# A graph network's second self connection, moved beside the edges of its layer

## The chip, the cores and the metric

The kernel runs on one core of a Trainium2 chip. The metric is the time on the device in microseconds (us), the median of several runs. The engines are called PE (TensorE, with its weight loads as PEld), DVE (VectorE), ACT (ScalarE), POOL (GpSimd) and SP (SyncE, which here only issues DMAs).

## The reference

A graph of 50,000 nodes with 160 features each (64 scalars, 32 vectors of 3) and 25,000 edges sorted by destination goes through two layers of a tensor product convolution. After each layer stands a residual and a layer norm. Cut to the second layer, which the change touches:

```python
sc = concatenate([x0 @ Wsc0 * a * inv8,
                  (einsum('num,uv->nvm', x1, Wsc1) * a[..., None] * inv32).reshape(n, 3 * MUL1)], axis=1)
f0, f1 = x0 @ Wl1_0 * a * inv8, einsum('num,uv->nvm', x1, Wl1_1) * a[..., None] * inv32
e0, e1 = f0[edge_src], f1[edge_src]
...                                     # messages from e0, e1 and the edge's weights, mean by destination
alpha = scal @ Wa * a * inv96
out_s = scal @ Wl2_s * a * inv96
out_v = einsum('num,uv->nvm', vec, Wl2_v) * a[..., None] * inv96
return sc + alpha * concatenate([out_s, out_v.reshape(n, 3 * MUL1)], axis=1)
...
x = layernorm(x + layer0(x)); x = layernorm(x + layer1(x))
```

The self connection `sc` needs only the layer's input x (in the kernel `x1_rows`, the output of the first layer) and the node's attribute `a`. So does the residual.

## The kernel before, in words

All numbers are fp32. The kernel has four stages, one after the other: edges of layer 0, nodes of layer 0, edges of layer 1, nodes of layer 1. An edge stage goes over 98 pairs of 128 edges, a node stage over 98 groups of 512 nodes (four node tiles of 128, `T = 4`).

The helper `run_stages` (line 59) writes out the order of every engine by hand: for each step k it calls a list of functions, each with its lag, so that `(3, second_map)` handles pair k - 3. The engines take their lists strictly in order and meet only in semaphores.

An edge stage, for pair j:

- SP loads the source indices, the edge scalars and the row of destinations (`load_src`, `load_attr`, `load_dst_row`); in layer 0 it also clears the table of layer 1 in `clear_table1` (L366).
- POOL gathers the source rows with two indirect DMAs (`gather`, L438). Seven steps later it adds the pair's sums into a table in HBM with two indirect DMAs that accumulate (`scatter`, L453). A scatter waits until the previous pair's scatter has landed, because the two can hit the same row.
- PE turns the gathered rows (`turn_x`, L526, L527), maps them (`first_map`, L542, L543), makes the edge's weights (`hidden`, `edge_weights`, L550), turns the products (`turn_mid`, L559), maps them (`second_map`, L573, L575, in layer 0 also L578) and sums edges of equal destination (`sum_pair`, L590 to L592).
- ACT copies out of PSUM (`copy_sums` is L710). DVE makes the products (`products`, L807 and on) and compares destinations. In `choose_rows` (L883, L884, in layer 1 L886) it picks the row to add to, for which it waits until the scatter of two pairs before has landed.

The node stage of layer 1, for group g: SP loads four tiles of x1 (`load_x1`) and of the table (`load_table`). ACT brings z together (`copy_z1`, L729). PE turns x1 (`turn1`, L627, L628) and multiplies it with the self weights (`nodes1`, in `self_connection`, L603 and L605). ACT copies the turned tiles (L735, L736). DVE adds the self connection times `a` to x1 (L930, four a group), takes the reciprocal of the edge count, adds the table's part (`table_row1`, L944) and takes statistics (`stats_of`, L952). POOL makes the factor (`factor`, L493 to L497) and the norm's scale and shift (`powers`, L470 to L485, 10 small operations of 128x4 elements). ACT normalises (L743) and stores `y`.

The buffers of x1 are a ring of four (`x1g`). Between the stages stands one wait for all stores of x1 (`s_store`): on POOL ahead of its first gather of layer 1, and on SP ahead of the last stage's loads.

## Time and profile before

| | us |
|---|---|
| median of 3 runs | 2438.08 |
| lowest and highest | 2436.28 and 2440.83 |
| span of the profiled execution, first to last instruction | 2446.7 |
| POOL busy in it | 1751.4 (72%) |
| PE busy | 1726.5 (71%) |
| DVE busy | 1506.3 (62%) |
| ACT busy | 1070.8 (44%) |

The profiled execution is its own run; its time is the span, some 8.6 us above the median of the runs. The profile names each instruction by engine, line and the tensors that it writes and reads. "Idle before, releaser" is the time in which the engine did nothing ahead of an instruction, and whose semaphore ended it. Matmuls are pipelined and their ends are modelled, so that a busy PE is not PE at its peak. PEclk is the TensorE clock that the chip granted, as a share of full speed (1.0 is 2.4 GHz, 0.5 is 1.2 GHz). The layer 0 edges run to about 860 us, its nodes to 1302, the layer 1 edges to about 2018 and its nodes to the end.

### The profile page before, as it was taken

The numbers are of one execution on the slowest core, as the hardware profiler recorded it, in microseconds if no ns is written. First come the engines' busy times: TensorE is split into PE (matmuls) and PEld (weight loads), VectorE is DVE, ScalarE is ACT, GpSimd is POOL, SyncE is SP. The second block draws the span as 40 slices with busy tenths as digits, with TensorE's granted clock in tenths as the row PEclk, the third lists the DMA queues.
The fourth block names the chain that finished last, engine by engine and source line by source line (L and its number), as shares of the span: only waits on it lengthen the run. The fifth ranks groups of instructions, "written<-read, shape, count | busy, mean of one in ns | idle before, by whom it ended". The sixth has DMA issues, their size and how long they took to land. (4 is left out here: it accounts for less than half of the span.)

```text
span 2446.7 us, 50266 instructions
## 1 busy us (share of the span) xinstructions
PE 1726.5 (71%) x10412; PEld 1528.8 (62%) x10412; DVE 1506.3 (62%) x6121; ACT 1070.8 (44%) x3336; POOL 1751.4 (72%) x3148
## 2 busy tenths in 40 slices
PE   0478888888888666666665878678777766666664
PEld 0367776777776566666664767567666655556564
DVE  1266666666666468888883444444444427888886
ACT  0233333333333246666663333333333325566665
POOL 1066677766667568888884777777777757888887
PEclk9988889888888788888875888988798878878877
DMA  5975555555555467777772444444444436666664
GB/s 223 422 198 121 117 117 117 119 117 116 118 118 119 77 202 252 240 244 243 240 221 69 71 67 69 70 70 69 69 68 69 70 53 226 234 232 235 230 236 175
DMA packets 270387, 374.52 MB, mean 153 GB/s; under 512 B 62544, under 2 KB 172944, under 8 KB 267280
## 3 DMA queue, kind: packets, MB, share of 16 engines
q1 hardware_dynamic: 163264, 203.38, 28.8%
q0 software_dynamic: 75264, 67.79, 19.3%
q10 hardware_dynamic: 31824, 102.97, 10.4%
q8 instruction: 11, 0.18, 0.0%
q14 instruction: 24, 0.20, 0.0%
HBM read 202.83 MB, written 171.16 MB: 153 GB/s over the span
## 5 line engine op out<-in xcount | busy, mean ns | idle before, releaser
L453 POOL DMA_INDIRECT table<-sums,row_i x392 | 632.9, 1615 | 307.0 <-ACT sums L710 104.1
L743 ACT ACTIVATE y<-res,shift,rstd 128x160 f32<-128x160 f32 x784 | 343.8, 509 | 307.4 <-POOL shift L485 307.3
L695 ACT COPY msg<-ps 128x192 f32<-128x192 f32 (+1 forms) x196 | 57.4, 293 | 620.3 <-PE ps L592 437.1
L438 POOL DMA_INDIRECT xg<-in_x_rows,src_i x196 | 199.3, 1017 | 172.2 <-DMA src_i<-in_src_col 69.7
L603 PE MATMUL ps<-self_m,xT 128*128 128x160 f32 (+1 forms) x1568 | 303.8, 350 | 7.6 <-DVE tab L901 4.6
L526 PE MATMUL ps<-ident,xg 128*128 128x128 f32 x392 | 94.1, 325 | 293.1 <-ACT xz L682 214.8
L603 PEld LDWEIGHTS ps<-self_m,xT 128*128 128x128 f32 x1568 | 266.7, 239 | 17.2 <-issue 5.3
L526 PEld LDWEIGHTS ps<-ident,xg 128*128 128x128 f32 x392 | 42.3, 151 | 353.6 <-ACT xz L682 194.4
L438 POOL DMA_INDIRECT xg<-x_rows,src_i x196 | 195.5, 997 | 70.8 <-issue 62.9
L573 PE MATMUL ps<-mapA,midT 128*128 128x128 f32 (+1 forms) x784 | 189.1, 329 | 50.3 <-DVE msg L848 47.8
L483 POOL TENSOR_TENSOR rstd<-var_e,minus_half 128x4 f32<-128x4 f32 x196 | 203.7, 1039 | 15.4
L952 DVE BATCH_NORM_STATS2 stats<-res 128x6 f32<-128x160 f32 x784 | 194.8, 308 | 6.1 <-POOL shift L485 6.0
L573 PEld LDWEIGHTS ps<-mapA,midT 128*128 128x128 f32 x784 | 145.2, 231 | 72.1 <-issue 64.4
L807 DVE TENSOR_TENSOR prod<-hs,ea_all 128x192 f32<-128x192 f32 x196 | 70.2, 358 | 184.5 <-ACT hs L670 163.3
L575 PE MATMUL ps<-mapB,midT 128*128 128x96 f32 x784 | 177.4, 315 | 0.0
L627 PE MATMUL ps<-ident,x1g 128*128 128x128 f32 x392 | 74.9, 322 | 141.6 <-ACT x1z L729 133.7
L618 PE MATMUL ps<-ident,xT 128*128 128x128 f32 x392 | 73.7, 317 | 139.1 <-DVE res L916 138.9
L944 DVE SCALAR_TENSOR_TENSOR res<-tab,small,res 128x160 f32<-128x160 f32 x392 | 124.6, 379 | 69.8 <-POOL small L497 69.7
L886 DVE COPY row_i<-row_all 128x2 int32 (+1 forms) x98 | 17.5, 178 | 237.0 <-DMA table<-sums,row_i 234.9
L559 PE MATMUL ps<-ident,mid 128*128 128x128 f32 x784 | 154.9, 334 | 0.0
L575 PEld LDWEIGHTS ps<-mapB,midT 128*128 128x128 f32 x784 | 150.2, 238 | 0.0
L627 PEld LDWEIGHTS ps<-ident,x1g 128*128 128x128 f32 x392 | 48.5, 160 | 156.9 <-ACT x1z L729 105.6
(121 smaller groups left out, 5019.8 us busy)
## 6 DMA issues: line engine op xcount, KB each, us to landing
tab<-table SPq DMA_DIRECT2D x98, 384.0 KB, 4.2
table<-zeros ACTq DMA_DIRECT2D x24, 1536.0 KB
table<-zeros SPq DMA_DIRECT2D x98, 324.0 KB
tab<-table SPq DMA_DIRECT2D x98, 324.0 KB, 3.3
x_rows<-y ACTq DMA_DIRECT2D x98, 320.0 KB, 3.7
x1g<-x_rows SPq DMA_DIRECT2D x98, 320.0 KB
out_rows<-y ACTq DMA_DIRECT2D x98, 320.0 KB, 2.4
dst_row<-in_dst_row SPq DMA_DIRECT2D x196, 128.0 KB
```

The source lines that it names most:

```text
L438: pool.indirect_dma_start(out=xg[u][:, t, 0:width], out_offset=None, in_=rows, in_offset=bass.IndirectOffsetOnAxis(ap=src_i[u][:, t:t + 1] ...
L453: pool.indirect_dma_start(out=table[l], out_offset=bass.IndirectOffsetOnAxis(ap=row_i[u][:, t:t + 1], axis=0), in_=sums[u][:, t, 0:W], in_ ...
L483: tt(rstd[u][:, :], var_e[:, :], minus_half[:, :], ALU.pow).then_inc(s_rstd, 1)
L526: turn(xgT_ps[:, t, :], xg[u][:, t, 0:M], ident[:, :])
L559: last = turn(midT_ps[:, 2 * c + t, :], mid[u][:, t, c * P:(c + 1) * P], ident[:, :])
L573: mm(o_ps[l][:, t, 0:SO + V], midT[u][:, t, :], mapA[l][:, :], start=t == 0, stop=not L["cross"], skip_group_check=True)
L575: last = mm(o_ps[l][:, t, SO + V:SO + 4 * V], midT[u][:, 2 + t, :], mapB[l][:, :], start=False, stop=not L["cross"], skip_group_check=True)
L603: mm(o[:, t // 2, t % 2, 0:z], xT[u][:, t * P:(t + 1) * P], w_m[:, :], start=True, stop=True)
L627: turn(x1T_ps[u][:, t * P:(t + 1) * P], x1g[u][:, t, 0:M], ident[:, :])
L743: last = nc.scalar.activation(y[u][:, t, :], res[u][:, t, :], ACT.Identity, scale=rstd[u][:, t:t + 1], bias=shift[u][:, t:t + 1])
L944: last = stt(res[u][:, t, :], tab1[u][:, t, 1:161], small[u][:, t, 3:4], res[u][:, t, :], ALU.mult, ALU.add)
L952: last = nc.vector.bn_stats(stats[u][:, t, :], res[u][:, t, :])
```

## The change

The self connection of layer 1, and the residual x1 with it, moves from the last stage into the edge stage of layer 1. In that stage each step k now also handles one node group:

- SP loads x1 of group k (`load_x1`), and four steps later stores its base rows (`store_base`) into a new array `base_rows` in HBM. The load of group k waits until the store of group k - 4 has landed, since both use one buffer of the ring. SP's wait for the stores of x1 now stands ahead of this edge stage.
- ACT brings z together; PE turns and multiplies in two halves of a group (`turn1a`, `turn1b`, `nodes1a`, `nodes1b`) through smaller PSUM tiles; ACT copies the halves (`copy_nTa`, `copy_nTb`); DVE adds them to x1 in place (`add_self_a`, `add_self_b`).
- To free PSUM, the two matmuls of the edge's weights become one of 384 columns over both halves of the edges. `fc2_1` is now 384 wide and block diagonal, cleared first and scaled in four parts.
- The last stage loads the base rows (`load_base`) where it loaded x1. On DVE `residual1` becomes `mean_factor` (two small operations), and `table_row1` adds to the base rows. PE has no work in it, and its warming matmuls are gone.

```diff
@@ sync @@
+                def load_x1(g, m, u):
+                    v = u % 4
+                    wait_count(sp, s_bstore[v], landed(g - 4, first_of(v), 4))
+                    sp.sem_inc(s_sptick, 1)
+                    sp.dma_start(x1g[v][:, :, :].rearrange("p t c -> p (t c)"),
+                                 x1_rows[bass.ds(m * GROUP, GROUP), :].rearrange("(p t) c -> p (t c)", t=T)).then_inc(s_nxT[v], 32)
+                def store_base(g, m, u):
+                    v = u % 4
+                    sp.wait_ge(s_z1, 2 * (g + 1 - NG))
+                    sp.dma_start(base_rows[bass.ds(m * GROUP, GROUP), :].rearrange("(p t) c -> p (t c)", t=T),
+                                 x1g[v][:, :, :].rearrange("p t c -> p (t c)")).then_inc(s_bstore[v], 16)
...
-                run_stages(sp, base, NP, 10, [(0, load_src), (0, load_attr), (4, load_dst_row)] + [(4, clear_table1)] * (l == 0))
+                if l == 1:
+                    for u in range(4):
+                        sp.wait_ge(s_store[u], stored(NG, u))
+                run_stages(sp, base, NP, 10, [(0, load_src), (0, load_attr), (4, load_dst_row)] +
+                           ([(4, clear_table1)] if l == 0 else [(4, store_base), (0, load_x1)]))
...
-                    run_stages(sp, NG, NG, 10, [(0, load_x1), (2, load_table)])
+                    run_stages(sp, NG, NG, 10, [(0, load_base), (2, load_table)])
@@ tensor @@
+                        last = mm(w_ps[1].rearrange("p t c -> p (t c)"), hidT[u][:, :], fc2[1][:, :], start=True, stop=True)
...
+                def turn1(g, b, u):
+                    v = u % 4
+                    pe.wait_ge(s_nxT[v], landed(g, v, 4, 32))
+                    pe.wait_ge(s_x1z, g + 1 - NG)
+                    wait_count(pe, s_nTsb, 2 * (g - NG) + b)
+                    for t in range(2):
+                        turn(x1T_ps[:, t * P:(t + 1) * P], x1g[v][:, 2 * b + t, 0:M], ident[:, :])
+                    turn(z1T_ps, x1z[v][:, 2 * b:2 * b + 2, :], ident[:, :]).then_inc(s_nT, 1)
+                def nodes1(g, b, u):
+                    v = u % 4
+                    pe.wait_ge(s_nTsb, 2 * (g - NG) + b + 1)
+                    wait_count(pe, s_z1, 2 * (g - NG) + b)
+                    for t in range(2):
+                        q = slice((2 * b + t) * P, (2 * b + t + 1) * P)
+                        mm(n1_ps[:, t, 0:M], xT[v][:, q], self_m[1][:, :], start=True, stop=True)
+                    mm(n1_ps[:, :, M:D], z1T[v][:, b, :], self_z[1][0:2 * V, 0:2 * V], start=True, stop=True).then_inc(s_n1, 1)
...
+                    run_stages(pe, NP, NP, 10, [(1, first_map), (0, hidden), (1, edge_weights), (2, nodes1a), (0, turn_x),
+                                                (1, turn1a), (3, second_map), (2, turn_mid), (1, turn1b),
+                                                (2, nodes1b), (5, sum_pair)])
@@ scalar @@
+                    run_stages(act, NP, NP, 10, [(0, copy_z), (1, copy_h), (0, hidden_act), (0, copy_xT),
+                                                 (1, copy_nTa), (3, copy_message), (2, copy_midT), (0, copy_z1),
+                                                 (1, copy_nTb), (5, copy_sums)])
@@ vector @@
+                def add_self(g, m, b, u):
+                    v = u % 4
+                    dve.wait_ge(s_n1, 2 * (g - NG) + b + 1)
+                    for t in range(2):
+                        a = a_all[:, bass.ds(m, 1), 2 * b + t:2 * b + t + 1].rearrange("p g t -> p (g t)")
+                        last = stt(x1g[v][:, 2 * b + t, :], n1_ps[:, t, :], a, x1g[v][:, 2 * b + t, :], ALU.mult, ALU.add)
+                    last.then_inc(s_z1, 1)
...
-                        (4, message_vectors), (4, compare), (4, message_sum), (1, products), (5, choose_rows)])
+                        (4, message_vectors), (4, compare), (4, message_sum), (2, add_self_a), (1, products), (5, choose_rows), (2, add_self_b)])
...
-                    run_stages(dve, NG, NG, 6, [(0, residual1), (1, stats_of), (0, table_row1)])
+                    run_stages(dve, NG, NG, 6, [(0, mean_factor), (1, stats_of), (0, table_row1)])
```

## Rows read from the trace of the kernel before

**Rows 1.** Busy time of the engines in three stages, then PEclk, DMA share, GB/s.

```profile
core 0: us, PE busy (x) PEld busy (x) DVE busy (x) ACT busy (x) POOL busy (x), PEclk, DMA share, GB/s
150.00:850.00 700.00, 585.41 (x3569) 508.97 (x3567) 463.34 (x2292) 261.59 (x907) 483.16 (x365) 0.86 0.55 116
...
1350.00:1960.00 610.00, 468.12 (x2928) 412.48 (x2927) 285.61 (x1241) 228.25 (x796) 460.36 (x353) 0.86 0.47 69
2050.00:2400.00 350.00, 229.29 (x1408) 209.61 (x1409) 289.79 (x1159) 212.98 (x578) 294.24 (x1075) 0.80 0.68 233
```

**Rows 2.** Groups of instructions in 2050 to 2400: busy us, mean ns, idle before.

```profile
L930 DVE SCALAR_TENSOR_TENSOR res<-ps,a_all,x1g 128x160 f32<-128x160 f32 x332 | 108.5, 365 | 0.0
```

**Rows 3.** POOL's waits in 2050 to 2400: us in total, times, longest.

```profile
POOL small L493 <- issue: 4.8, 20, 0.2
```

**Rows 4.** Order of time in one group of the last stage: start, duration.

```profile
2200.36 0.20 POOL L493 TENSOR_TENSOR small<-a_all,small 128x4 f32<-128x4 f32 x1 [0.24 <-issue]
...
2201.25 1.27 DVE L944 SCALAR_TENSOR_TENSOR res<-tab,small,res 128x160 f32<-128x160 f32 x4 [0.92 <-POOL small L497]
...
2201.39 0.30 POOL L472 TENSOR_TENSOR squares<-stats 128x4 f32<-128x4 f32 x1
...
2201.95 0.36 POOL L475 TENSOR_SCALAR neg_mean<-mean 128x4 f32<-128x4 f32 x1
...
2204.53 0.21 POOL L493 TENSOR_TENSOR small<-a_all,small 128x4 f32<-128x4 f32 x1
```

**Rows 5.** Gathers in 150:850 and 1350:1960: duration, first and last start.

```profile
L438 POOL DMA_INDIRECT xg<-in_x_rows,src_i x177: 977/1019/1261, 149.1 to 810.1; - x177
...
L438 POOL DMA_INDIRECT xg<-x_rows,src_i x177: 977/1017/1032, 1349.3 to 1959.1; - x177
```

**Rows 6.** Order of time in one pair of the layer 1 edges.

```profile
1602.97 1.64 POOL L453 DMA_INDIRECT table<-sums,row_i  x1 [0.56 <-issue]
...
1604.91 1.59 POOL L453 DMA_INDIRECT table<-sums,row_i  x1 [0.30 <-PE ps L527]
...
1609.05 0.17 DVE L886 COPY row_i<-row_all 128x2 int32 x1 [2.20 <-DMA table<-sums,row_i]
...
1609.87 1.62 POOL L453 DMA_INDIRECT table<-sums,row_i  x1 [0.76 <-ACT sums L710]
...
1611.11 0.44 PE L526 MATMUL ps<-ident,xg 128*128 128x128 f32 x2 [0.71 <-DMA xg<-x_rows,src_i]
```

**Rows 7.** Busy times as in rows 1, in single pairs and groups.

```profile
1548.44:1555.49 7.05, 4.43 (x33) 3.82 (x33) 3.06 (x14) 2.59 (x10) 5.45 (x5) 1.00 0.43 68
1687.41:1694.73 7.32, 7.31 (x33) 6.64 (x33) 3.13 (x14) 2.90 (x11) 5.42 (x5) 0.57 0.44 65
2206.64:2210.84 4.20, 2.19 (x17) 1.95 (x18) 3.54 (x16) 2.51 (x8) 3.59 (x14) 1.00 0.69 246
2181.05:2185.22 4.17, 3.78 (x17) 3.60 (x17) 3.25 (x15) 2.58 (x8) 3.38 (x13) 0.50 0.68 231
...
426.31:435.60 9.29, 8.71 (x39) 7.79 (x39) 6.19 (x31) 3.17 (x12) 6.39 (x6) 0.63 0.48 98
```

**Rows 8.** Order of time in one pair of the layer 0 edges.

```profile
502.57 1.59 POOL L453 DMA_INDIRECT table<-sums,row_i  x1 [0.31 <-issue]
...
503.03 0.35 SPq L366 DMA_DIRECT2D table<-zeros  x1
...
507.44 0.16 DVE L883 TENSOR_TENSOR row_i<-step,dst_f 128x2 int32<-128x2 f32 x1 [1.52 <-DMA table<-sums,row_i]
...
508.34 1.62 POOL L453 DMA_INDIRECT table<-sums,row_i  x1 [1.56 <-DVE row_all L884]
```

**Rows 9.** DMA issues: KB each, median us from issue to landing.

```profile
tab<-table SPq DMA_DIRECT2D x98, 324.0 KB, 3.3
...
out_rows<-y ACTq DMA_DIRECT2D x98, 320.0 KB, 2.4
```

**Rows 10.** Order of time at two starts: of the layer 1 edges, of ACT.

```profile
91.83 1.28 ACT L682 ACT_TABLE_LOAD   x1 [91.83 <-issue]
...
1304.98 1.11 POOL L438 DMA_INDIRECT xg<-x_rows,src_i  x1 [4.98 <-DMA x_rows<-y]
```

130 lines of the change are left out of this document (71 added, 59 removed).

## The prediction

> **What bounds the kernel now.** I read first the busy time by stage, then the waits, then the order of time inside a stage. The kernel has four stages, one after the other: edges and nodes of the first layer, edges and nodes of the second. The change takes work out of the fourth and puts it into the third, so the questions are what sets the pace of each.
>
> The last stage runs at 4.22 us a group: 332 runs of L930, four a group, in 350 us [rows 2]. POOL is shown 84% busy, and in those 350 us it waits 4.8 us in all, for nothing that another engine does [rows 1, 3]. Its 13 small operations follow each other from one L493 to the next in 4.17 us [rows 4]; each step waits for the one before on POOL itself, so the time between them belongs to the chain. DVE's L944 waits 0.92 us for POOL's L497 in that group [rows 4]. POOL is the bound, and it touches nothing of the self connection.
>
> The third stage runs at 6.93 us a pair (176 starts of L438, two a pair, from 1349.3 to 1959.1) [rows 5]. It is a closed loop over the scatters: the two scatters of a pair take POOL from 1602.97 to 1606.50, 3.53 us; DVE sees them landed at 1609.05, 2.55 later; the next pair's first scatter starts at 1609.87, 0.82 after that [rows 6]. That is 6.90. The two gathers and their gaps lie inside the wait for the landing. PE is not the bound at full clock: one pair's 33 matmuls take 4.43 us. In a pair at clock 0.57 they take 7.31 of 7.32, all of it [rows 7]. The first layer's edges show the same loop with more traffic: the second scatter ends at 504.16, its landing is seen 3.28 later, the next starts 0.90 after that [rows 8], 7.7 with the 3.5 on POOL; its mean is 7.51 [rows 5].
>
> **Taken out of the last stage.** On DVE four L930 a group, 108.5 us in 350 or 1.31 a group; on PE five transposes and six matmuls, all of its 229.29 us, 2.76 a group; on ACT three copies, within the 2.57 us a group that it is busy in all [rows 1, 2]. All of it ran beside POOL's chain, so it buys nothing in steady state. Could POOL's steps get shorter? L472 takes 0.29 and L475 0.36 where L493 takes 0.20, and beside both runs L944, from 2201.25 for 1.27, not L930 [rows 4]. L944 stays, at the same place behind L497. I take 0; the gain is bounded by those two and the 0.25 us they are over, 24 us in 98 groups. Only the fill of the first group gets shorter, by at most the 1.31 us of its L930: I take -1. The transfers are as before, 320 KB of base rows for 320 KB of x1. The warming matmuls of this stage lay behind the last scatters and go for nothing.
>
> **Added to the third stage, DMA.** Each pair gets a load of 320 KB and a store of 320 KB. The last stage moves three such transfers a group at a DMA share of 0.68 [rows 1], so one is 0.68 x 4.22 / 3 = 0.96 us of all 16 DMA engines. Two are 1.9, on 0.47 x 6.93 = 3.3 now. The total of 5.2 fits in a pair; what counts is how much of it stands in front of a scatter's landing. Nearest row: the first layer's edges, where SP issues 324 KB of zeros (L366) at 503.03, beside the second scatter [rows 8], and the mean pair is 7.51 - 6.93 = 0.58 longer. Part of that may be its wider table rows. The new order is no kinder. The base store needs add_self_b, which on DVE stands behind choose_rows, and that waits for a landing. So the store is issued 0.9 us after a landing, with the next scatter. The load of x1 waits for that store (2.4 us to landing for out_rows [rows 9]), so it starts about 3.5 us into the loop, when the second scatter is out, and the next dst_row follows. Bounds: 0.3 us a pair (half of the first layer's surplus) and 1.9 (all of both in front). I take 0.9, one and a half times the first layer's surplus for twice the bytes. The loop is then 7.8.
>
> The Trainium skill ("DMA: Bandwidth & Descriptors", "Queues, rings and completion order") says that each DMA engine takes the queues with work in turn, a packet at a time. By that rule a scatter packet can be kept waiting by a packet of x1 or base, and the sum would go towards the upper bound, 8.8 us a pair; the first layer's longer landing agrees in sign. It is one more reason against the change, and no term is taken from it.
>
> **Added to the third stage, PE.** Six transposes and six matmuls, in the records 18 against 17 before (a matmul is two, a transpose one): 2.19 us a group at full clock, 3.78 at 0.50 [rows 7]. The edge weights become one matmul over both halves, 384 columns for 2 x 192: the same columns and two weight loads fewer, 0 (0.1 at most). So a pair costs 4.43 + 2.19 = 6.62 us at full clock. From the two rows of each, a lower clock adds (7.31 - 4.43)/0.43 = 6.7 and (3.78 - 2.19)/0.5 = 3.2 us per unit: 6.62 + 9.9 x (1 - clock). The stages stand at 0.80 to 0.86, higher in both edge stages, where PE is busier [rows 1]. At 0.86 the pair costs 8.0, at full clock 6.6. I take 0.92, between them, since PE's gaps shrink: 7.4. That is under the loop's 7.8, but not by much, and a pair at half clock (11.6) runs past it, as in the first layer, where a pair at 0.63 took 9.29 us with PE busy for 8.71 [rows 7]. For this I add 0.1.
>
> The Trainium skill ("TensorE: Matmul & The Clock Gate", Part 1) says that the array drops to half clock after it sat idle and comes back with sustained work. By that rule the fuller third stage would stay at full clock and the PE term would vanish, which is the second rival. The trace gives it only half support: in the first layer PE is busy for 84% and stands at 0.86 as well.
>
> **Added to the third stage, other engines.** DVE gets 1.3 us on 3.06 a pair; ACT gets five copies for three, which even at the 2.57 of a whole group are less than the 4.3 that it has free beside its 2.59; POOL gets nothing [rows 1, 2, 7]. The waits: PE's nodes1a waits for add_self_b of the group before, 0.9 us behind the landing, with turn_x queued behind it. The gather that turn_x needs lands 2.06 us behind the same landing (1609.05 to 1611.11 [rows 6]), and nodes1a's 0.8 (6 of 17 records of 2.19 us) fits between. ACT's copy_z1 waits for x1, with copy_sums, which a scatter needs, queued behind: x1 is there 0.9 + 2.4 + 3.3 us and two issues of 0.35, so 7.3, after the landing two pairs earlier [rows 8, 9], where two periods less one microsecond, some 13, are free. SP now blocks for the base store with load_src behind it; sources are loaded three pairs ahead, so one pair's delay is covered. If that cover goes, x1 is late next, and then the scatter.
>
> At the start of the stage SP now waits for all x1 stores before it loads the first sources; POOL had started its gather the moment the stores had landed, at 1304.98 [rows 10]. The load of the sources takes 0.35 to issue and at most what a store takes, 2.4, to land [rows 8, 9]: between 0.4 and 2.8, I take +2. The wider fc2 costs DVE a clear and two scalings at the start, where ACT first acts at 91.8 us, behind its own DMA issues [rows 10]: 0, and 1 at most.
>
> **Sum.** Period 7.8 + 0.1 = 7.9 for 6.93, +0.97 over 97 pairs is +94; +2 - 1. The profiled span of 2446.7 becomes 2542. The median of the runs is 8.6 below that span, so 2438.1 + 95 = 2533 us.
>
> **The rivals.**
> - *The two transfers cost what the one cost in the first layer, and PE's clock holds.* Period 7.2 to 7.6, 7.45 in the middle: 2438 + 51 + 1 = 2490. For it: the last stage carries its three transfers without a stall. Against: there nothing waits for a scatter.
> - *PE becomes the bound, or x1 comes late.* At a clock of 0.86 the pair costs 8.0, and with stalls on top 8.2 to 8.9: 2562 to 2630. For it: 0.86 with PE busy for 84% in the first layer. Against: PE would have almost no gap left.
> - *Faster.* The steps L472 and L475 are long because DVE and POOL get in each other's way, and with 1.31 us less DVE work a group they fall to 0.20: -24 us. It decides if the third stage grows by less than 0.24 us a pair. Against: L944, which stays, is what runs beside them.
> - *No difference.* Both transfers fall beside the gathers and the loop stays at 6.9: 2439.
>
> **How the numbers follow.** Forecast (period 7.6 to 8.2, 2504 to 2562) 0.56; transfers cheap 0.19; PE or x1 bound 0.15; faster 0.05; no difference 0.05. A measurement here can tell some 0.2%, 5 us, from no change. Range 2470 to 2600: from a period of 7.25, inside the first rival, to 8.6, inside the second. Below it stay the two cases without growth and a little of the first rival, 0.12; above it 0.07 of the second. Faster 0.05, same 0.05, slower 0.90.
>
> **What would show it.** Last stage: POOL from L493 to L493 still 4.17, DVE's busy share down by a third, PE idle. Third stage: gathers 7.9 us a pair apart; scatter to landing 3.3 to 3.6 us where it was 2.55; DMA share about 0.65; PE over 90% busy; clock 0.9 or more. Wrong if the landing stays at 2.5, if the last stage's POOL chain shortens by more than 0.1 us, or if POOL's scatters wait mostly for ACT's sums and not for landings (then PE or x1 is the bound).

## The result, and the profile after

| | before | after |
|---|---|---|
| median of 4 runs each, us | 2439.45 | 2475.10 |
| lowest and highest | 2436.28, 2445.26 | 2466.02, 2481.67 |
| ratio, with its 95% interval | | 1.0142 (1.0116 to 1.0169) |
| span of the profiled execution | 2446.7 | 2464.3 |

The change costs 35.7 us. The forecast was slower by 95 us: the sign was right, the size 2.7 times too large. Its range began at 2470, so that 2475.1 lies at its low end.

The two profiled executions are 17.6 us apart and not 35.7. The span of before, 2446.7, is longer than any of its four runs (2436.28 to 2445.26), and that of after belongs to the fastest of its four (2466.02). The other 18 us are in runs without a profile, and the traces below can't place them.

Busy times by stage of after, in the columns of [rows 1]:

```profile
core 0: us, PE busy (x) PEld busy (x) DVE busy (x) ACT busy (x) POOL busy (x), PEclk, DMA share, GB/s
1350.00:1960.00 610.00, 610.00 (x4195) 529.08 (x4193) 374.66 (x1543) 294.63 (x1194) 446.58 (x342) 1.00 0.71 159
2050.00:2400.00 350.00, 0.00 (x0) 0.00 (x0) 216.77 (x837) 145.52 (x332) 293.88 (x1086) 0.50 0.69 235
```

In the layer 1 edges PE is busy for all of the 610 us, at the full clock. In [rows 1] it was 468 at 0.86. No other number of this row matters as much: a stage in which PE has no gap takes the time of its matmuls. The DMA share went from 0.47 to 0.71.

The accumulating scatters of the layer 1 edges, before and then after (duration, first and last start):

```profile
L453 POOL DMA_INDIRECT table<-sums,row_i x196: 1552/1618/1761, 1345.5 to 2016.5; - x196
```

```profile
L471 POOL DMA_INDIRECT table<-sums,row_i x196: 1552/1587/1780, 1350.1 to 2039.0; - x196
```

From the first to the last start it is 671.0 us before and 688.9 after, +17.9. With two more rows the whole profiled difference is placed. Order of time on POOL at the start of the stage in after, as in [rows 10]:

```profile
1296.21 0.20 POOL L503 TENSOR_TENSOR shift<-neg_mean,rstd 128x4 f32<-128x4 f32 x1
1303.23 1.11 POOL L456 DMA_INDIRECT xg<-x_rows,src_i  x1 [6.82 <-issue]
```

- First gather: 1304.98 [rows 10] and 1303.23, -1.75.
- First gather to first scatter, the fill of the stage: 1345.5 - 1304.98 = 40.5 and 1350.1 - 1303.23 = 46.9, +6.3.
- The 196 scatters: +17.9.
- Last scatter to the end: 2446.7 - 2016.5 = 430.2 and 2464.3 - 2039.0 = 425.3, -4.9.

The sum is +17.6. The fill is a term that the forecast did not have. Its size is rough: the edge stage of the kernel before stands again in e10 and e13 below, with fills of 35.0 and 41.6, and the changed one in e15, with 46.6.

One pair of the layer 1 edges in after, order of time, as in [rows 6] (SPq is SP issuing a DMA):

```profile
1599.74 0.27 PE L545 MATMUL ps<-ident,xz 128*64 128x128 f32 x1
...
1600.85 1.62 POOL L471 DMA_INDIRECT table<-sums,row_i  x1 [1.05 <-DMA table<-sums,row_i]
...
1602.77 1.58 POOL L471 DMA_INDIRECT table<-sums,row_i  x1 [0.30 <-DMA src_i<-in_src_col]
1602.94 0.68 DVE L949 SCALAR_TENSOR_TENSOR x1g<-ps,a_all,x1g 128x160 f32<-128x160 f32 x2 [0.67 <-PE ps L633]
...
1603.79 0.35 SPq L381 DMA_DIRECT2D base_rows<-x1g  x1
...
1604.95 0.91 PE L571 MATMUL ps<-fc,hidT 128*128 128x384 f32 x2
...
1605.70 0.61 PE L632 MATMUL ps<-self_m,xT 128*128 128x128 f32 x4
...
1606.24 0.43 PE L633 MATMUL ps<-self_z,z1T 64*128 64x64 f32 x2
1606.60 0.20 PEld L544 LDWEIGHTS ps<-ident,xg 128*128 128x128 f32 x2
...
1606.79 0.36 SPq L374 DMA_DIRECT2D x1g<-x_rows  x1
...
1606.88 0.27 PE L545 MATMUL ps<-ident,xz 128*64 128x128 f32 x1
...
1607.88 1.64 POOL L471 DMA_INDIRECT table<-sums,row_i  x1 [0.91 <-DMA table<-sums,row_i]
...
1609.24 0.24 DVE L941 COPY row_i<-row_all 128x2 int32 x1
```

The same PE instruction, L545, comes back after 1606.88 - 1599.74 = 7.14 us. No PE row has idle time in front of it. POOL's first scatter does wait for the landing of the pair before (0.91 us at 1607.88), so both are near their limit; which of them sets the pace is a question for the experiments. DVE's L941 no longer waits for a landing (in [rows 6] its twin L886 did, 2.20 us). The base store goes out at 1603.79, 2.94 us after the pair's first scatter, as soon as L949 ends at 1603.62. The load of x1 follows at 1606.79, 5.94 after that scatter. The view of SP's waits in 1350 to 1960 says what it stood for:

```profile
SPq L373 <- DMA base_rows<-x1g: 218.9, 84, 5.0
SPq L381 <- DVE x1g L949: 125.2, 81, 2.5
```

One group of the last stage of after, as in [rows 4], and POOL's only wait in 2050 to 2400, as in [rows 3]:

```profile
2203.12 0.21 POOL L511 TENSOR_TENSOR small<-a_all,small 128x4 f32<-128x4 f32 x1 [0.24 <-issue]
...
2204.08 1.27 DVE L1003 SCALAR_TENSOR_TENSOR res<-tab,small,x1g 128x160 f32<-128x160 f32 x4 [1.71 <-POOL small L515]
2204.15 0.38 POOL L490 TENSOR_TENSOR squares<-stats 128x4 f32<-128x4 f32 x1
...
2204.78 0.36 POOL L493 TENSOR_SCALAR neg_mean<-mean 128x4 f32<-128x4 f32 x1
...
2207.38 0.21 POOL L511 TENSOR_TENSOR small<-a_all,small 128x4 f32<-128x4 f32 x1
```

```profile
POOL small L511 <- issue: 4.5, 19, 0.2
```

From L511 to L511 it is 4.26 in this group, which has a short `issue` gap in front. Over the stage POOL's L501 starts 53 times from 2101.0 to 2319.1, 4.19 a group, against 4.23 of its twin L483 (52 times, 2101.6 to 2317.3). PE is idle, DVE went from 290 to 217 busy, and POOL's chain is what it was.

### The profile page after: what moved, and what is told of

The parts are those of the page before. It is cut to its first block and busy times, and to the rows that moved or that the text cites. A ratio compares the mean times of both kernels' runs of the same rounds, so it can differ in the third digit from the quotient of the medians.

```text
span 2464.3 us, 51498 instructions
## 1 busy us (share of the span) xinstructions
PE 1623.4 (66%) x10302; PEld 1420.8 (58%) x10302; DVE 1527.7 (62%) x6124; ACT 1077.3 (44%) x3532; POOL 1748.8 (71%) x3148
## 5 line engine op out<-in xcount | busy, mean ns | idle before, releaser
L949 DVE SCALAR_TENSOR_TENSOR x1g<-ps,a_all,x1g 128x160 f32<-128x160 f32 x392 | 132.4, 379 | 203.4 <-PE ps L633 202.7
L501 POOL TENSOR_TENSOR rstd<-var_e,minus_half 128x4 f32<-128x4 f32 x196 | 204.2, 1042 | 15.4
L1003 DVE SCALAR_TENSOR_TENSOR res<-tab,small,x1g 128x160 f32<-128x160 f32 x392 | 127.0, 381 | 136.2 <-issue 97.2
L544 PE MATMUL ps<-ident,xg 128*128 128x128 f32 x392 | 88.1, 307 | 134.5 <-ACT xz L724 120.6
L661 PE MATMUL ps<-self_m,xT 128*128 128x160 f32 x784 | 162.4, 364 | 4.8 <-DVE tab L971 4.8
L596 PE MATMUL ps<-mapB,midT 128*128 128x96 f32 x784 | 156.8, 284 | 0.0
L661 PEld LDWEIGHTS ps<-self_m,xT 128*128 128x128 f32 x784 | 143.8, 239 | 6.3 <-issue 5.5
L898 DVE TENSOR_TENSOR pe<-ps,ea_all 128x192 f32<-128x192 f32 x196 | 70.1, 358 | 116.5 <-ACT msg L737 104.5
L544 PEld LDWEIGHTS ps<-ident,xg 128*128 128x128 f32 x392 | 40.4, 144 | 174.4 <-ACT xz L724 89.2
L552 PE MATMUL ps<-attrT,fc 128*128 128x128 f32 (+1 forms) x392 | 97.3, 330 | 58.8 <-DVE self_z L824 34.5
L676 PEld LDWEIGHTS ps<-ident,xT 128*128 128x128 f32 x392 | 48.1, 159 | 151.9 <-DVE res L986 151.7
L580 PE MATMUL ps<-ident,mid 128*128 128x128 f32 x784 | 135.1, 301 | 0.0
L596 PEld LDWEIGHTS ps<-mapB,midT 128*128 128x128 f32 x784 | 130.1, 208 | 0.0
```

The lines of the kernel that those rows point to most:

```text
L501: tt(rstd[u][:, :], var_e[:, :], minus_half[:, :], ALU.pow).then_inc(s_rstd, 1)
L544: turn(xgT_ps[:, t, :], xg[u][:, t, 0:M], ident[:, :])
L552: mm(hidT_ps, fc1[l][0:R2, :], attrT[u][0:R2, :], start=True, stop=True).then_inc(s_hid, 1)
L580: last = turn(midT_ps[:, 2 * c + t, :], mid[u][:, t, c * P:(c + 1) * P], ident[:, :])
L596: last = mm(o_ps[l][:, t, SO + V:SO + 4 * V], midT[u][:, 2 + t, :], mapB[l][:, :], start=False, stop=not L["cross"], skip_group_check=True)
L661: mm(o[:, t // 2, t % 2, 0:z], xT[u][:, t * P:(t + 1) * P], w_m[:, :], start=True, stop=True)
```

## The experiments

All runs in one table. "Pair" is the mean distance of the middle pairs of the layer 1 edges, from the starts of the gathers. "Landing" is the mean time from the end of a pair's second scatter to its completion in the trace. The two scatters take 3.5 us, and the next first scatter follows 0.9 us after the landing where it waits for nothing else. What a pair has beyond these sums is another wait: 0.2 to 0.4 us in e4, e9, e11 and e12, 0.5 to 0.8 in e2, e6, e8, e14 and e16. "Group" is the mean of the last stage. Ratios are to the kernel before, run in turn on the same chip (its medians there 2439.9, 2444.0, 2444.0 and 2444.9).

| run | median us | ratio (95%) | pair | landing | group |
|---|---|---|---|---|---|
| before | 2439.5 | | 6.93 | 2.40 | 4.23 |
| after | 2475.1 | 1.014 (1.012 to 1.017) | 7.14 | 2.67 | 4.19 |
| e1_transfers | 2473.9 | 1.011 (1.007 to 1.016) | 7.29 | 2.89 | 4.24 |
| e11_transfers_other_place | 2427.2 | 0.993 (0.991 to 0.995) | 6.74 | 2.01 | 4.23 |
| e2_matmuls | 2457.4 | 1.008 (1.006 to 1.009) | 7.02 | 1.86 | 4.23 |
| e7_merged | 2444.2 | 1.001 (1.000 to 1.003) | 6.93 | 2.50 | 4.24 |
| e6_cut | 2470.6 | 1.012 (1.008 to 1.016) | 7.14 | 2.01 | 4.19 |
| e16_cut_again | 2467.5 | 1.011 (1.007 to 1.014) | 7.14 | 2.00 | 4.17 |
| e4_z_once | 2452.0 | 1.002 (1.000 to 1.004) | 6.96 | 2.28 | 4.17 |
| e17_z_once_cut | 2410.3 | 0.987 (0.983 to 0.991) | 6.54 | 2.10 | 4.17 |
| e18_dst_row_last | 2501.9 | 1.025 (1.021 to 1.029) | 7.48 | 3.04 | 4.17 |
| e14_after_again | 2505.6 | 1.025 (1.021 to 1.030) | 7.56 | 2.42 | 4.18 |
| e15_after_third | 2473.1 | 1.013 (1.009 to 1.016) | 7.12 | 2.67 | 4.19 |
| e10_before_dve_factor | 2428.8 | 0.993 (0.990 to 0.996) | 6.91 | 2.36 | 4.10 |
| e13_before_table_early | 2430.5 | 0.994 (0.992 to 0.996) | 6.91 | 2.36 | 4.09 |
| e8_dve_factor | 2468.0 | 1.013 (1.007 to 1.019) | 7.39 | 2.48 | 3.88 |
| e9_dve_factor_z_once | 2422.3 | 0.992 (0.989 to 0.995) | 6.95 | 2.26 | 3.91 |
| e12_table_early | 2360.8 | 0.967 (0.964 to 0.969) | 6.94 | 2.15 | 3.30 |

A row's pair, landing and group come from one execution, its median from several. The layer 0 edges, which no edit touches, show how much one execution can differ: from the first to the last scatter they took 723.6 us in the profile of before, 729.4 in that of e4_z_once, 711.6 in that of e8_dve_factor and 699.3 in that of e11_transfers_other_place.

### The transfers alone

The kernel before, with the load of x1 and a store of the same rows beside the layer 1 edges. What it stores is x1 itself, and the last stage still loads x1.

```diff
+                def load_early(g, m, u):
+                    v = u % 4
+                    wait_count(sp, s_bstore[v], landed(g - 4, first_of(v), 4))
+                    sp.sem_inc(s_sptick, 1)
+                    sp.dma_start(x1g[v][:, :, :].rearrange("p t c -> p (t c)"),
+                                 x1_rows[bass.ds(m * GROUP, GROUP), :].rearrange("(p t) c -> p (t c)", t=T)).then_inc(s_xl[v], 16)
+                def store_early(g, m, u):
+                    v = u % 4
+                    wait_count(sp, s_row, g - 2)
+                    sp.wait_ge(s_xl[v], landed(g, first_of(v), 4))
+                    sp.dma_start(base_rows[bass.ds(m * GROUP, GROUP), :].rearrange("(p t) c -> p (t c)", t=T),
+                                 x1g[v][:, :, :].rearrange("p t c -> p (t c)")).then_inc(s_bstore[v], 16)
...
-                run_stages(sp, base, NP, 10, [(0, load_src), (0, load_attr), (4, load_dst_row)] + [(4, clear_table1)] * (l == 0))
+                run_stages(sp, base, NP, 10, [(0, load_src), (0, load_attr), (4, load_dst_row)] +
+                           ([(4, clear_table1)] if l == 0 else [(4, store_early), (0, load_early)]))
```

> The kernel before with only the two transfers added to the layer 1 edges: x1 is loaded and stored to base_rows at the places in SP's order that the change gives them, and used by nothing; the last stage is as before. Theory A (PE sets the new pace, the transfers cost little): a pair grows by no more than the 0.25 us by which the landing grew in the changed kernel, so 2440 + 2 + 0 to 25, some 2450, and the clock stays near 0.86. Rival B (the step of the forecast: the transfers stand in front of the scatters' landings): a pair at 7.4 to 7.8 us and 2490 to 2525, and the changed kernel's PE is busy all the time only because it is spread out to that pace.

Measured: 2473.9 us, a pair of 7.29, between the theory and the rival and in neither's range. The landing comes 2.89 us after the second scatter, for 2.40 before. PE is not the bound here: in 1350 to 1960 it is busy for 458.56 of 610 us at clock 0.83. So the transfers without any matmul cost nearly what the whole change costs.

e11_transfers_other_place drops one line of it, the wait for DVE's `row_i`. The bytes are the same.

```diff
                 def store_early(g, m, u):
-                    wait_count(sp, s_row, g - 2)
                     sp.wait_ge(s_xl[v], landed(g, first_of(v), 4))
```

> The transfers alone, as in e1_transfers, but the base store no longer waits for a landing; SP is then paced by the gathers, and by the order of its queue the store should go out 2.7 us after the first scatter of a pair and the x1 load about 5.7 us after it, where the changed kernel has them (3.2 and 6.0); in e1_transfers they stood at 6.9 and 2.3. If it is the place of the transfers and not their bytes that delays a landing: the landing falls from 2.89 us to 2.4 to 2.6, the pair from 7.29 to 6.95 to 7.1, 2445 to 2457. If it is the bytes: 7.3 and 2470 to 2476 again.

Measured: 2427.2 us, faster than the kernel before by 0.7%, and below the range that I had for the place. The profiled execution is the fastest of its ten (2405.3 us), and its layer 0 edges are 24 us shorter than those of before, so its pair of 6.74 and its landing of 2.01 flatter the edit. The medians of e1 and e11 do not hang on it: 47 us, or 0.48 a pair, for one wait. The order of time shows where the bytes went. First e1_transfers, then e11_transfers_other_place:

```profile
1602.03 1.62 POOL L481 DMA_INDIRECT table<-sums,row_i  x1 [1.69 <-ACT sums L738]
1603.95 1.67 POOL L481 DMA_INDIRECT table<-sums,row_i  x1 [0.30 <-PE ps L555]
1604.09 0.33 SPq L382 DMA_DIRECT2D x1g<-x_rows  x1
...
1609.11 0.17 DVE L914 COPY row_i<-row_all 128x2 int32 x1 [3.37 <-DMA table<-sums,row_i]
```

```profile
1605.78 1.58 POOL L480 DMA_INDIRECT table<-sums,row_i  x1 [0.30 <-issue]
...
1608.41 0.33 SPq L382 DMA_DIRECT2D x1g<-x_rows  x1
...
1609.46 0.17 DVE L913 COPY row_i<-row_all 128x2 int32 x1 [3.00 <-DMA table<-sums,row_i]
```

In the first, x1 is issued at 1604.09, beside the second scatter, and the landing is seen at 1609.11, 3.49 after that scatter's end at 1605.62. In the second, x1 is issued 1.05 us after the scatter's end at 1607.36, and the landing is seen 2.10 after it. By the medians of all pairs, counted from a pair's first scatter, x1 went out at 2.3 us in e1, at 5.1 in e11 and at 6.0 in the changed kernel; the base store at 6.9, 1.4 and 3.2; the destination rows (128 KB) at 4.1, 0.9 and 1.1, where before it was 2.1. The same bytes had different prices by their place. The forecast had one price for the bytes. The size counts as well where the place is bad: in e17_z_once_cut below, x1 goes out at 2.2 us and the destination rows at 4.0, as in e1, but x1 has 80 KB for 320 (and so has the base store, at 0.3), and the landing is 2.10 for 2.89.

### The matmuls alone

The kernel before, with the change's six transposes and six matmuls a pair in their new places, on tiles of weights and old data. Their results are used by nothing, and the last stage stays as it was.

```diff
+                    run_stages(pe, NP, NP, 10, [(1, first_map), (0, hidden), (1, edge_weights), (2, spare_maps), (0, turn_x),
+                                                (1, spare_turns), (3, second_map), (2, turn_mid), (1, spare_turns),
+                                                (2, spare_maps), (5, sum_pair)])
```

> The kernel before with only PE work added to the layer 1 edges: per pair the same 6 transposes and 6 matmuls of the same shapes at the same places in PE's order, from a tile that lies ready into an unused PSUM bank, without a new wait; their results are used by nothing. The two matmuls of the edge weights stay two. Theory A: PE is busy nearly all the time, the clock there goes to 1.0 as in the changed kernel, and the pair comes to 6.9 to 7.0, since PE's own 6.7 to 6.8 us now lie just under the scatters' loop: 2440 to 2450. Rival C (a fuller PE alone costs nothing, the new waits between PE, ACT and DVE do): pair unchanged, PE with gaps of 0.5 us or more, 2440. Rival D (the clock still falls): mean clock 0.9 to 0.95 there and 2470 or more.

Measured: 2457.4 us, slower than my theory's range, a pair of 7.02, PE busy for 610.00 of 610.00 us at clock 1.00. The landing got shorter, 1.86, and the next scatter starts 1.6 us after it and not 0.9: it waits for ACT's sums, which wait for PE. PE alone is a bound of its own here, with the edge's weights still in two matmuls.

e7_merged has only the merged edge weights in the kernel before:

```diff
-                    for t in range(2):
-                        q = slice(t * H, (t + 1) * H)
-                        last = mm(w_ps[l][:, t, :], hidT[u][q, :], fc2[l][q, :], start=True, stop=True)
+                        last = mm(w_ps[1].rearrange("p t c -> p (t c)"), hidT[u][:, :], fc2[1][:, :], start=True, stop=True)
```

> The kernel before with only the merged edge weights of layer 1: one matmul of 384 columns over both halves in place of two of 192 columns with 64 rows each. By the forecast it costs PE 0 to 0.1 us a pair less. Theory A: it costs about 0.3 us more (in the traces the group took 0.60 us before and 0.91 after), because the two small ones ran side by side in different rows of the array: the PE time of a pair at full clock goes from 4.43 to 4.7, and since PE is not the bound there, the time changes by less than 5 us, 2436 to 2445.

Measured: 2444.2 us, no difference, since PE is not the bound there. But PE's work grew. A single pair at full clock, in the columns of [rows 7], where it was 4.43:

```profile
1364.08:1371.30 7.22, 4.74 (x32) 3.82 (x32) 3.16 (x14) 2.59 (x10) 5.45 (x5) 1.00 0.49 66
```

The order of time of e2_matmuls shows the form with two matmuls:

```profile
1602.18 0.60 PE L550 MATMUL ps<-fc,hidT 64*128 64x192 f32 x4
1602.70 0.71 PE L603 MATMUL ps<-self_m,xT 128*128 128x128 f32 x4
1603.34 0.43 PE L604 MATMUL ps<-self_z,xT 64*128 64x64 f32 x2
```

There the next work starts 0.52 us after L550. After the merged L571 it starts 0.75 us later (1604.95 and 1605.70 in the pair of after). But L603, behind L550, has 0.64 us to its next work, and L632, behind L571, has 0.54. So "the same columns" cost 0.23 - 0.10 = 0.13 us more where maps of the self connection follow, and the two pairs in which PE has no gap say the same: 7.14 for 7.02. Where a gap follows, as in e7, it is 4.74 - 4.43 = 0.31. Two matmuls over 64 rows each took less time than one over 128 rows with as many columns in all.

e4_z_once changes the other half of the added work: z of a group is turned once, as one 128-row tile, and multiplied over 128 rows with the weights of its half, which are zero elsewhere.

```diff
-                    turn(z1T_ps, x1z[v][:, 2 * b:2 * b + 2, :], ident[:, :]).then_inc(s_nT, 1)
+                    if b == 0:
+                        last = turn(z1T_ps, x1z[v][:, :, :], ident[:, :])
+                    last.then_inc(s_nT, 1)
...
-                    mm(n1_ps[:, :, M:D], z1T[v][:, b, :], self_z[1][0:2 * V, 0:2 * V], start=True, stop=True).then_inc(s_n1, 1)
+                    mm(n1_ps[:, :, M:D], z1T[v][:, :], self_z[1][:, b * 2 * V:(b + 1) * 2 * V], start=True, stop=True).then_inc(s_n1, 1)
```

> The changed kernel with z turned once a group: one transpose of 128 columns of z and one copy in the first half, and the z matmul of each half over all 128 rows, where there were two transposes, two copies and matmuls over 64 rows. One PE record less a pair and no switch to 64 rows there. Theory A (PE sets 7.14 us a pair): PE falls to 6.8 to 6.9 a pair and the pair with it, down to the scatters' loop at about 7.0 to 7.1: 2460 to 2470. Rival B (the transfers' loop stands right behind PE): PE gets gaps, the clock may fall again, and the pair stays at 7.1 to 7.3 as with the transfers alone (7.29): 2470 to 2490.

Measured: 2452.0 us, a pair of 6.96, under the ranges of both. PE is busy for 579.14 of 610 us and no longer the bound all the time. The landing is 2.28, and from it to the next first scatter it is 1.15 us where 0.93 is usual: DVE comes to `row_i` (L945) 0.26 us after the landing in the median, for 0.11 in e17. What holds DVE in these pairs was not tried. The same matmuls without a gap stand in e17_z_once_cut, below.

### The transfers cut, then both eased

e6_cut is the changed kernel with a quarter of the bytes (its expectation says what it leaves out); e16_cut_again is the same kernel in a later measurement.

```diff
-                    sp.dma_start(x1g[v][:, :, :].rearrange("p t c -> p (t c)"),
-                                 x1_rows[bass.ds(m * GROUP, GROUP), :].rearrange("(p t) c -> p (t c)", t=T)).then_inc(s_nxT[v], 32)
+                    n = T if isinstance(m, int) and m < 4 else 1
+                    sp.dma_start(x1g[v][:, 0:n, :].rearrange("p t c -> p (t c)"),
+                                 x1_rows[bass.ds(m * GROUP, GROUP), :].rearrange("(p t) c -> p (t c)", t=T)[:, 0:n * D]).then_inc(s_nxT[v], 32)
...
-                                 x1g[v][:, :, :].rearrange("p t c -> p (t c)")).then_inc(s_bstore[v], 16)
+                                 x1g[v][:, 0:1, :].rearrange("p t c -> p (t c)")).then_inc(s_bstore[v], 16)
```

> The changed kernel with its x1 load and its base store in the layer 1 edges cut to one node tile of four (80 KB each for 320 KB), and the last stage loading x1_rows where it loaded base_rows; so only a part of the self connection reaches the output, while every engine's work is as in the changed kernel. Theory A: PE still sets 7.14 us a pair, 2470 to 2476. Rival B: the pair falls to 6.9 to 7.0 and PE gets gaps, 2450 to 2458.

> The changed kernel with its x1 load and base store in the edge stage cut to a quarter (one node tile of four; the last stage loads x1 itself), again, beside the changed kernel on one chip. Theory: the gaps on TensorE come from late transfers, so with little to transfer the pair is 7.14 us in this measurement as in the first (2470.6 us), within 5 us of that, whatever the whole kernel shows beside it. Rival: the gaps have nothing to do with the bytes, and this kernel shows them as well (7.3 to 7.6 us a pair, over 2485 us).

Measured: 2470.6 and 2467.5 us, both with a pair of 7.14 and PE busy for 610.00 of 610.00 us. The landing came earlier, 2.0 for 2.67, and the time went into waiting for ACT's sums. In the changed kernel the bytes are hidden: the pair is PE's 7.14 with all of them or with a quarter.

e17_z_once_cut puts e4_z_once and e6_cut together, so both costs shrink at once.

> The changed kernel with z turned once a group and both transfers cut to a quarter (the last stage loads x1 itself): both costs are made smaller at once. Theory of two limits close together: TensorE's 6.55 us at full clock is then under the transfers' loop as well as under 7.14, and the loop is shorter by the cut's 0.6 us of landing, so the pair is 6.6 to 6.8 us and the time 2425 to 2445, under the 2452.0 with z once alone. Rival (one bound, TensorE alone): the pair stays at 6.9 to 7.0 as with z once alone.

Measured: 2410.3 us, a pair of 6.54, below what I expected. A single pair of it, in the columns of [rows 7], and the order of time on PE in another, and on POOL:

```profile
1362.36:1368.72 6.36, 6.36 (x50) 5.79 (x50) 4.34 (x18) 3.33 (x14) 5.14 (x5) 1.00 0.54 100
```

```profile
1602.89 0.61 PE L635 MATMUL ps<-self_m,xT 128*128 128x128 f32 x4
1603.34 0.33 PE L636 MATMUL ps<-self_z,z1T 128*128 128x64 f32 x2
1603.53 0.44 PE L545 MATMUL ps<-ident,xg 128*128 128x128 f32 x2
```

```profile
1601.30 1.62 POOL L472 DMA_INDIRECT table<-sums,row_i  x1 [0.30 <-issue]
1603.23 1.58 POOL L472 DMA_INDIRECT table<-sums,row_i  x1 [0.30 <-issue]
1605.11 1.02 POOL L457 DMA_INDIRECT xg<-x_rows,src_i  x1 [0.31 <-issue]
1606.43 0.98 POOL L457 DMA_INDIRECT xg<-x_rows,src_i  x1 [0.30 <-issue]
1607.71 1.62 POOL L472 DMA_INDIRECT table<-sums,row_i  x1 [0.30 <-issue]
```

With z once, PE's pair without a gap is 6.36 us for 7.14. The rows say why. A half of the self connection takes 0.45 + 0.19 = 0.64 from start to start here, and 0.54 + 0.36 = 0.90 in the pair of after (L632 at 1605.70, L633 at 1606.24, L544 at 1606.60). That is 0.52 for two halves; one z transpose less makes up 0.11 more, so 0.63 of the 0.78. The scatter loop now is 3.53 + 2.10 + 0.93 = 6.56, which is the measured pair. But the landing is not what most of these pairs wait for. POOL's two scatters and two gathers follow each other with the 0.30 us that stands ahead of every one of them, and come back after 1607.71 - 1601.30 = 6.41 us. In 1350 to 1960, 58 of 89 first scatters have at most 0.36 us in front. POOL's own four transfers, some 6.43 us, are a third limit, which neither my expectation nor the forecast had: the gathers fit into the wait for the landing only as long as it is longer than they are.

So two limits stood close together in the changed kernel: PE's 7.14, and the scatter loop at 3.53 + 2.67 + 0.92 = 7.12. With z once alone the pair was 6.96, though PE could do 6.36; with the cut alone it stayed at 7.14; only both gave 6.54.

e18_dst_row_last keeps everything of the changed kernel but SP's order:

```diff
-                run_stages(sp, base, NP, 10, [(0, load_src), (0, load_attr), (4, load_dst_row)] +
-                           ([(4, clear_table1)] if l == 0 else [(4, store_base), (0, load_x1)]))
+                    run_stages(sp, base, NP, 10, [(4, store_base), (0, load_src), (0, load_attr), (0, load_x1), (4, load_dst_row)])
```

> The changed kernel with the same transfers in another order on SyncE: base store, sources, edge scalars, x1, and only then the destination row, where it was sources, edge scalars, destination row, base store, x1. Theory: at 7.14 us a pair TensorE is the bound, so where the bytes stand in the loop moves the landing (2.0 to 2.9 us after the second scatter) and not the period: 7.14, 2465 to 2480 us. Rival: the place of the bytes sets the period as it did with the transfers alone (6.74 against 7.29 us): 7.4 or more, over 2490 us.

Measured: 2501.9 us, a pair of 7.48, so my theory for it was wrong and its rival right. Order of time:

```profile
1604.55 1.59 POOL L473 DMA_INDIRECT table<-sums,row_i  x1 [0.30 <-PE ps L547]
1605.43 0.36 SPq L374 DMA_DIRECT2D x1g<-x_rows  x1
1605.98 0.33 SPq L362 DMA_DIRECT2D dst_row<-in_dst_row  x1
...
1609.10 0.17 DVE L943 COPY row_i<-row_all 128x2 int32 x1 [2.46 <-DMA table<-sums,row_i]
```

x1 and the destination rows go out beside the second scatter, and the landing comes 3.04 us after its end in the mean. Both moved at once, so what each of them costs is not separated. The loop is 3.53 + 3.04 + 0.92 = 7.49, above PE's 7.14, and it sets the pair. That is a third of a microsecond on a pair, 30 us in 98, from the order of one list.

### The changed kernel again

e14_after_again and e15_after_third are the changed kernel as it is.

> The changed kernel again, on the chip and beside the runs of the others, since its runs spread from 2466 to 2482 and e8, which differs from it only in the last stage, had 7.39 us a pair in the edges where it had 7.14. Expected 2465 to 2485, 7.1 to 7.4 a pair; PE busy all the time at 7.14, gaps in it where a pair takes longer.

> The changed kernel a third time, as it is, beside three others on one chip. Its two measurements so far were 2475.1 us (an edge pair of 7.14 us, TensorE without a gap) and 2505.55 us (7.56 us, gaps of some 24 us in the stage, all ahead of the second turn of x1). If the difference is chance of the run, it lies anywhere from 2466 to 2515 and its pair is 7.14 plus its gaps.

Measured: 2505.6 (2495.0 to 2515.0) and 2473.1 us (2468.6 to 2478.6). e15_after_third repeats the first result (pair 7.12, landing 2.67). e14_after_again is 30 us slower, above the 2485 that I had as the most, and its waits in 1350 to 1960 have one that after and e15_after_third have not:

```profile
PE ps L622 <- ACT z1T L767: 18.4, 20, 2.0
```

L622 is `turn1b`, which writes the PSUM tile that ACT's `copy_nTa` must first have read. In the pair of after, ACT is done with it at 1601.01 and PE comes at 1601.48: a slack of 0.5 us. In e14_after_again ACT is late by more, in some 20 pairs. The order of time of one of them:

```profile
1573.87 0.37 ACT L766 COPY xT<-ps 128x256 f32<-128x256 f32 x1 [1.80 <-remote]
1574.14 0.26 ACT L767 COPY z1T<-ps 64x128 f32<-64x128 f32 x1
...
1574.45 0.44 PE L622 MATMUL ps<-ident,x1g 128*128 128x128 f32 x2 [2.02 <-ACT z1T L767]
```

"remote" is a release of which the records do not show the origin, so what held ACT for 1.80 us stays open. e8_dve_factor, whose edges are those of the changed kernel, has the same wait 9 times and a pair of 7.39. The versions with a quarter of the bytes never showed such a gap, in two measurements; but these edges did not either, in two of four, so that the gaps come with the transfers is not shown.

### What the last stage could give

The forecast said that POOL's chain is the bound there and that the change buys nothing from it. If that is right, three steps of `factor` taken from POOL and given to DVE must shorten a group, and more so where DVE has been relieved.

```diff
-                    run_stages(pool, NG, NG, 6, [(0, factor), (1, powers)])
+                    run_stages(pool, NG, NG, 6, [(1, powers)])
...
-                    run_stages(dve, NG, NG, 6, [(0, mean_factor), (1, stats_of), (0, table_row1)])
+                    run_stages(dve, NG, NG, 6, [(0, mean_factor), (1, stats_of), (0, factor), (0, table_row1)])
```

e8_dve_factor is this in the changed kernel, e9_dve_factor_z_once the same with z turned once, e10_before_dve_factor in the kernel before.

> The changed kernel with the three small operations of factor moved from POOL to DVE in the last stage, behind the statistics. If POOL's own chain is the bound there (4.17 us, of which these three steps are 0.73), the group falls to 3.45 to 3.55 us: 98 x 0.65 to 0.7 is 64 to 69 us, some 2408. Rival: DVE (2.6 us a group, with these and their waits some 3.4) or the three transfers (2.9 us of the DMA engines a group) become the bound at 3.8 to 4.0: 2440 to 2455. If the last stage were bound by something else than POOL, nothing changes: 2474.

> Both of the others in one kernel. They touch different stages, so the gains should add: by theory A 2395 to 2405, by rival B for the edges 2405 to 2420. Either way faster than both kernels.

> The kernel before with the same three operations moved from POOL to DVE. DVE has 3.5 us of work a group there, with these about 4.1 and their waits 4.2 to 4.3: the bound goes from POOL to DVE and the time stays, 2435 to 2450. Rival: DVE's work overlaps better than that and the group falls to 3.8, 2405: then the change was not needed to make the room.

Measured, by group: 3.88, 3.91 and 4.10, where it was 4.19 in the changed kernel and 4.23 in the kernel before. So POOL's chain was the bound, and the next one came early, as the rivals had it. The times are 2468.0 us, with the slow edge pairs of 7.39, then 2422.3, just above the upper rival's range, and 2428.8, under the range expected. In the kernel before, what limits the group next is DVE itself; in e9 it is the table's load. The waits in 2050 to 2300, first of e10_before_dve_factor, then of e9_dve_factor_z_once:

```profile
POOL mean L470 <- DVE stats L963: 39.6, 61, 0.7
```

```profile
DVE small L997 <- DMA tab<-table: 44.5, 52, 1.8
```

So the table was then loaded two groups earlier, in both:

```diff
-                    run_stages(sp, NG, NG, 10, [(0, load_base), (2, load_table)])
+                    run_stages(sp, NG, NG, 10, [(0, load_base), (0, load_table)])
```

> The same for the kernel before with the factor on DVE (e10, 4.10 us a group). DVE was the bound there, with nearly no wait for the table: 4.0 to 4.1 a group and 2420 to 2430. If it falls to 3.6 as in e12, the move of the self connection was not needed.

> e9_dve_factor_z_once with the table's load of the last stage issued right behind the base load of the same group (lag 0 for 2). In e8 and e9 DVE waited 51 us in 300 for that load, and a group took 3.9 us. If that wait is the rest above POOL's ten steps (3.45), the group falls to 3.5 to 3.6: 30 to 40 us less than e9, 2382 to 2392. If the three transfers' volume is the bound, it stays at 3.9 and 2422.

Measured: 2430.5 us in the kernel before (group 4.09, nothing gained from the load) and 2360.8 in the changed one (group 3.30, under my 3.5 to 3.6). Busy times of the last stage, in the columns of [rows 1], of e13_before_table_early and then of e12_table_early:

```profile
2050.00:2340.00 290.00, 188.94 (x1205) 171.65 (x1204) 277.12 (x1205) 182.82 (x496) 211.47 (x709) 0.84 0.76 242
```

```profile
2050.00:2340.00 290.00, 0.00 (x0) 0.00 (x0) 258.20 (x1144) 154.33 (x352) 245.59 (x880) 0.50 0.87 299
```

With the self connection in this stage DVE is busy for 277 of 290 us once it also makes the factor: 277.1 x 4.09 / 290 = 3.91 us a group, and that is the end of it. Without the self connection it is 258.2 x 3.30 / 290 = 2.94 us a group, and the group goes down until DVE (89% busy) and POOL (85%) are both near full. POOL's ten steps are close to the bound again: in these 290 us POOL waits for no other engine and has 4.1 us of `issue`. The change is worth 4.09 - 3.30 = 0.79 us a group, 77 us in 98 (70 between the medians, with the edges' part), but only together with the two edits that use the room it makes. e12_table_early is the fastest kernel here: 3.3% under the kernel before.

## Why the prediction was right or wrong

**What bounds before: right, with a floor close below.** The pair was the sum of the loop's three parts, 3.53 + 2.40 + 0.98 = 6.91 in the kernel before, and it moved with the landing where only bytes were moved (e1, e11), with PE's work unchanged. In e11 it moved by less (0.39 on the landing, 0.19 on the pair), since the third part grew to 1.20. 0.3 us more of PE work alone changed nothing (e7). POOL's own 6.43 lay half a microsecond under it, which the forecast did not say.

**Taken out of the last stage: right.** POOL's chain stayed (4.19 for 4.23 a group), L472 and L475 did not shorten (their twins take 0.38 and 0.36), and e10_before_dve_factor shows the chain as the bound by shortening it. From the last scatter to the end the gain was 4.9 us, where I took 1.

**Added, DMA: the step that failed.** I took +0.9 us a pair for a loop of 7.8. Measured were +0.27 on the landing in the changed kernel (2.40 to 2.67), where PE hides it, and +0.49 on the landing and +0.36 on the pair with the transfers alone (e1). The landing that I looked for at 3.3 to 3.6 us was 2.67. The step that was wrong is the placing. I let the base store wait for a landing, through `choose_rows`; but with a longer pair the scatter of two pairs before has long landed when DVE gets there (L941 without a wait), and `add_self_b` waits for PE's L633 instead. The store then goes out 3.2 us after the first scatter and x1 at 6.0, just before the next one, where neither stands in front of the landing by much. And I priced bytes, by the first layer's surplus, without their place: the same bytes gave pairs of 6.74 (e11, in its fastest execution), 7.29 (e1) and, with PE's work, 7.14 (after) and 7.48 (e18). Of my two bounds, 0.3 and 1.9, even the worst place came to 0.64 on the landing (2.40 to 3.04). The Trainium skill's rule on DMA engines that take their queues in turn ("DMA: Bandwidth & Descriptors", "Queues, rings and completion order") agrees in sign with the longer landing where a bulk transfer is issued beside the scatter (2.89 and 3.04 us for 2.40). A pair near the upper bound of 8.8, towards which I took it to point, did not come.

**Added, PE: total near, both parts off.** I had 6.62 at full clock and a clock of 0.92, for 7.4. Measured is 7.14 at clock 1.00. The full-clock work was 0.52 too low. With the edge's weights still in two matmuls, PE's pair without a gap is 7.02 (e2), so the self connection in halves costs 7.02 - 4.43 = 2.59 for the 2.19 that I took from the last stage. Of it 2 x 0.33 are its turns and 2 x 0.90 its maps, start to start in the pair of after. There `self_connection` maps z over 128 rows (L605), in the change over 64: the rows that I priced it by were not of the same shape. The merged edge weights cost another 7.14 - 7.02 = 0.12 where I said nothing, and at most 0.1 less. 4.43 + 2.59 + 0.12 = 7.14. The clock penalty, in turn, was not there, nor the 0.1 for pairs at half clock: full clock for 610 us with PE busy all the time, as in e2_matmuls and e6_cut, against 0.86 with PE busy for 77% before. Here the Trainium skill's rule ("TensorE: Matmul & The Clock Gate", Part 1), that sustained work brings the full clock and idling loses it, came out, and my half-way value between it and the trace did not. The forecast set that rule beside the second rival; it belongs to the first, in which the clock holds.

**The bound: wrong side.** I took the loop as the bound at 7.8 and PE's 7.4 under it. It is PE at 7.14, with the loop just under it at 7.12: three quarters of the bytes less left the pair at 7.14 (e6, e16). The first rival, with cheap transfers and a held clock, asked for 7.2 to 7.6 and 2490 us; it is the nearest, and gave the low end. The sum by my own steps with the measured terms: pair 7.14 for 6.93 over 97 pairs is +20, fill +6, start +2, last stage -5, so +23, against the 17.6 between the profiles (whose layer 0 happened to end 3.6 us earlier, and whose last pairs are shorter) and the 35.7 between the medians.

**Start: right.** From POOL's last small step to the first gather it is 1303.23 - 1296.21 = 7.0 us, where it was 1304.98 - 1299.80 = 5.2 (L485 to L438): +1.8 for the 2 that I took. What I left out is the fill: +6.3 us until the first scatter in these two executions.

**Open.** Why ACT is late in some executions of the changed kernel (30 us in e14_after_again), and with it the part of the 35.7 us that the profile of after does not hold. Why e11_transfers_other_place beats the kernel before: in it the destination rows go out at 0.9 us and not at 2.1, which fits, but it was not tried by itself. What delays DVE after the landing in e4, e9 and e12, whose pairs stay at 6.9 with PE and POOL both able to do 6.4, was not tried either.

## What to carry to other kernels

When work moves into a stage with a closed loop over DMAs, work out the loop, the fullest engine and the issuing engine's own sequence, and expect the largest, with the engine's work taken from rows of the very same shapes. Price a bulk transfer by where it is issued against the transfer that the loop waits for, and not by its bytes alone. Look at an unchanged stage of each profile before trusting a small difference in a changed one. Relieving an engine off the critical path is worth nothing until work on the path is given to it: here three steps given to DVE, with z turned once and an earlier load, made a loss of 1.4% a gain of 3.3%.

## What the runs showed of the hardware

- Two matmuls of 64 rows and 192 columns each took 0.52 us until the next work, and one of 128 rows and 384 columns 0.75; the map behind took 0.64 and 0.54, so that a pair grew by 0.12 (e2, after). Two maps over 128 rows and one of z over 64 took 0.90 us, the same with z over 128 rows and zeros in the weights 0.64 (after, e17). Fewer instructions were not less time.
- With 320 KB more in each direction a pair, the landing of an accumulating scatter was anything between 2.01 and 3.04 us, by the place, where it was 2.40 without them. The 2.01 is from an execution that was fast in other stages too.
- POOL's indirect DMAs have 0.30 us between them at the least. Two scatters and two gathers of 128 rows then take 6.4 us, and the mean pair stayed above that where nothing else held it for long (6.54 in e17).
- In the layer 1 edges PE had a mean clock of 0.83 to 0.88 where it was busy for 75 to 79% (before, e1, e7, e10), at 0.99 with 95% (e4_z_once), and at 1.00 with 100%. With no work on PE the last stage shows 0.50.
- Two POOL steps are longer than the 0.20 us of the others. In the means of 2050 to 2300 they took 0.29 and 0.36 us before (L472, L475), and 0.27 and 0.35 when DVE had lost its self connection (L490, L493 of after). In e12_table_early the same L493 took 0.23, and the step of L501 1.09 for 1.04; what lengthens them was not tried.
